# One buffer or two, by parity of the chunk, for the input of a depthwise convolution

## The reference, cut to what matters

```
zxbcdt = u @ in_w.T                       # 512 -> 1024 (z) + 1152 (xBC) + 16 (dt)
z, xBC, dt = split(zxbcdt)
xBC = conv1d(xBC, conv_w, depthwise, 4 taps, causal) + conv_b
xBC = silu(xBC)
xh, B, C = split(xBC)                     # 1024, 64, 64
state = dA * state + (dt * x) B^T;  y = C state      # per token, 16 heads of 64
y = (y + D * xh) * silu(z);  y = y * rsqrt(mean(y*y) + EPS) * rms_w
h = h + y @ out_w.T
```

## Time and profile before

| | us | share |
|---|---|---|
| median of three runs | 4825.02 | |
| profiled execution | 4828.47 | |
| its span | 4826.7 | |
| TensorE matmuls busy | 4096.1 | 85% |
| TensorE weight loads busy | 3622.3 | 75% |
| VectorE busy | 3357.0 | 70% |
| ScalarE busy | 2922.8 | 61% |
| GpSimd busy | 2002.1 | 41% |

### The profile page before, as it was taken

One profiled execution on the slowest core, in us unless ns is written; L12 is line 12 of the kernel. 1 busy time (PEld: TensorE's weight loads), 2 busy tenths in 40 slices (PEclk: granted clock), 3 DMA queues, 4 the chain that ended last, 5 costly groups with the idle time before them and its releaser, 6 DMA issues. The chain is left out here.

```text
span 4826.7 us, 100096 instructions
## 1 busy us (share of the span) xinstructions
PE 4096.1 (85%) x38872; PEld 3622.3 (75%) x38872; DVE 3357.0 (70%) x5217; ACT 2922.8 (61%) x4904; POOL 2002.1 (41%) x1572
## 2 busy tenths in 40 slices
PE   4399888888889899956989898989898998499999
PEld 1388888888878788846878888888888888377777
DVE  7377777777777777745777777777777777466664
ACT  4466666666666666635666666666666666466664
POOL 7134333333333334421333343434343444466664
PEclk6699999999999999978999999999999999699999
DMA  8300000000000000020000000000000000322220
GB/s 310 105 27 28 28 28 28 28 28 28 28 28 28 28 28 28 23 73 26 28 28 27 28 27 28 27 28 27 28 27 28 27 29 28 110 83 88 83 87 36
DMA packets 108673, 220.99 MB, mean 46 GB/s; under 512 B 10760, under 2 KB 11272, under 8 KB 107272
## 3 DMA queue, kind: packets, MB, share of 16 engines
q1 hardware_dynamic: 108176, 214.25, 12.6%
HBM read 146.97 MB, written 67.24 MB: 44 GB/s over the span
## 5 line engine op out<-in xcount | busy, mean ns | idle before, releaser
L501 PE MATMUL l_ring<-l_u_hi,l_wi_lo 128*128 128x256 f32 x4608 | 1312.9, 285 | 81.0 <-ACT l_raw L742 72.4
L501 PE MATMUL l_ring<-l_u_lo,l_wi_hi 128*128 128x256 f32 x4608 | 1298.1, 282 | 0.0
L501 PE MATMUL l_ring<-l_u_hi,l_wi_hi 128*128 128x256 f32 x4608 | 1296.9, 281 | 0.0
L974 DVE SCALAR_TENSOR_TENSOR l_xc<-l_raw,l_prm,l_xc 128x256 f32<-128x256 f32 x1536 | 852.3, 596 | 232.6 <-ACT l_xc L751 214.4
L501 PEld LDWEIGHTS l_ring<-l_u_hi,l_wi_lo 128*128 128x128 f32 x4608 | 876.4, 190 | 105.7 <-ACT l_raw L742 85.9
L501 PEld LDWEIGHTS l_ring<-l_u_lo,l_wi_hi 128*128 128x128 f32 x4608 | 876.1, 190 | 8.9
L501 PEld LDWEIGHTS l_ring<-l_u_hi,l_wi_hi 128*128 128x128 f32 x4608 | 874.6, 190 | 0.0
L1149 POOL TENSOR_TENSOR l_g<-l_g 128x512 f32<-128x512 f32 (+2 forms) x384 | 347.0, 904 | 926.8 <-ACT l_g L812 906.7
L1120 POOL TENSOR_TENSOR l_rhs<-l_cum,l_small 32x1024 fp32r<-32x1024 f32 x256 | 496.3, 1939 | 514.8 <-PE l_wide L563 474.1
L1006 DVE TENSOR_TENSOR l_e<-l_e,l_ps_m 128x1024 f32<-128x1024 f32 x256 | 312.8, 1222 | 414.2 <-ACT l_e L800 410.2
L501 PE MATMUL l_ring<-l_wo_hi,l_g_lo 128*128 128x512 f32 x1024 | 411.9, 402 | 82.9 <-DVE l_g_lo L1026 82.9
(11 more groups left out here) (162 smaller groups left out, 8335.2 us busy)
## 6 DMA issues: line engine op xcount, KB each, us to landing
l_hn<-h_scratch SPq DMA_DIRECT2D x64, 512.0 KB, 4.0
l_res<-h_scratch SPq DMA_DIRECT2D x128, 256.0 KB, 3.8
h_scratch<-l_res SPq DMA_DIRECT2D x128, 256.0 KB, 2.1
m_rows<-in_x SPq DMA_DIRECT2D x16, 1024.0 KB, 9.5
h_scratch<-m_rows SPq DMA_DIRECT2D x16, 1024.0 KB, 7.7
f_x<-in_x SPq DMA_DIRECT2D x16, 1024.0 KB, 6.1
f_h<-h_scratch SPq DMA_DIRECT2D x16, 1024.0 KB, 8.2
out<-f_x SPq DMA_DIRECT2D x64, 256.0 KB, 2.0
```

Source lines behind the costliest of these rows:

```text
L501: last = nc.tensor.matmul(out, a, c, start=(k == 0), stop=(k == n - 1))
L974: ins = nc.vector.scalar_tensor_tensor(out=acc, in0=raw[:, k, tap:tap + TB], scalar=prm_sb[:, w:w + 1], in1=acc, op0=ALU.mult, op1=ALU.add)
```

## The change

`raw` gets a dimension of two ahead of the others: [128, 2, 2, 259]. A chunk uses the half `(s + c) % 2`. As a step has five chunks and a sequence four steps, this is the parity of m, so neighbouring chunks have different halves. `conv_in` waits for `s_acc >= m - 1`, the taps of the chunk before the last, in place of `s_acc >= m`. Nothing else is changed: the order on each engine and all other waits stay.

```diff
-        raw = sb("raw", [P, 2, TB + TAPS - 1])
+        raw = sb("raw", [P, 2, 2, TB + TAPS - 1])
...
-                act.wait_ge(s_acc, m)
+                act.wait_ge(s_acc, at_least_0(m - 1))
                 if s == 0:
-                    nc.scalar.mul(raw[:, 0:nt, 0:TAPS - 1], small[:, 0:nt * 3].rearrange("p (k t) -> p k t", k=nt),
+                    nc.scalar.mul(raw[:, (s + c) % 2, 0:nt, 0:TAPS - 1], small[:, 0:nt * 3].rearrange("p (k t) -> p k t", k=nt),
                                   0.0).then_inc(s_halo, 1)
                 else:
                     act.wait_ge(s_halo2, m - (NX + 1) + 1)
-                    nc.scalar.copy(raw[:, 0:nt, 0:TAPS - 1], halo[:, t0:t0 + nt, :]).then_inc(s_halo, 1)
+                    nc.scalar.copy(raw[:, (s + c) % 2, 0:nt, 0:TAPS - 1], halo[:, t0:t0 + nt, :]).then_inc(s_halo, 1)
...
-                nc.scalar.copy(raw[:, 0:nt, TAPS - 1:], src_ps).then_inc(s_inev, 1)
+                nc.scalar.copy(raw[:, (s + c) % 2, 0:nt, TAPS - 1:], src_ps).then_inc(s_inev, 1)
...
-                    ins = nc.scalar.activation(acc_bc if c == 0 else xc[:, t0 - 1 + k, :], raw[:, k, 0:TB],
+                    ins = nc.scalar.activation(acc_bc if c == 0 else xc[:, t0 - 1 + k, :], raw[:, (s + c) % 2, k, 0:TB],
...
-                            out=acc, in0=raw[:, k, tap:tap + TB], scalar=prm_sb[:, w:w + 1], in1=acc,
+                            out=acc, in0=raw[:, (s + c) % 2, k, tap:tap + TB], scalar=prm_sb[:, w:w + 1], in1=acc,
```

## The result

Four runs of the changed kernel took 4616.07 to 4621.96 us, median 4619.05; four of the kernel before in the same comparison had 4825.90. The ratio is 0.957 (0.9555 to 0.9588): 207 us less. The prediction was 4633, the range 4612 to 4712. The profiled execution has a span of 4614.2 us, 212.5 less. The forecast's own narrower range, 4620 to 4652, misses the result by 1 us; what holds is the wider margin down to 4612.

The account below looks back on a forecast made before the run. No engine is full; raw's single buffer ties ScalarE and VectorE into a zigzag, with TensorE in the chain. Terms gave 2.85 to 3.2 us per step, taken as 3.1; 62 x 3.1 = 192 off 4825.0 gives 4633, range 4612 to 4712.

Parts of the forecast that it names:

- The wait attributed: ScalarE, chunks 3 and 4: conv_in waits for VectorE's taps (s_acc), though the view names TensorE; no size of its own.
- Chunk 2, 0.94 per step: conv_in starts 3.28 us earlier, so TensorE's wait before the states product goes: 0.94 us per step.
- Chunk 3, 1.10 per step: conv_in's copy comes earlier, so TensorE's wait before projection group 8 goes: 1.10 us per step.
- Chunk 4, 0.81: conv_in waits for group 8's end instead of taps 3: 1360.83 - 1360.02, within a start 3.0 us earlier.
- Sum: Whole kernel: 62 steps x 3.1 us = 192 us saved, from 4825.0 to 4633.
- upper bound of 3.2 per step: Highest gain per step: 3.0 by the transposes' start, plus about 0.1 for each of two TensorE restarts.
- Where it does not act: First step's chunks before each layer's loop (silu_x waits for the same taps) and each layer's last step: no gain.
- The lock: GpSimd and two-SBUF-input VectorE instructions share a port pair exclusively; the later blocks: 1.5 us for a caught tap.
- the addresses: Second buffer and tensors behind raw, moved 2072 bytes: cost taken as 0; slower reads feared, 5% chance, up to 4907.
- the register form of the wait: One more subtraction in the loop for conv_in's wait: at most some 0.1 us in chunk 2, taken as 0.
- Rival 2: Taps 4: one more tap waits for a GpSimd addition, 1.5 us more; step wins 1.6, 99 us, 4726; 7%.

Follow-up runs that it names:

- first experiment: Changed kernel with both halves of raw kept, but conv_in waiting again for the taps of the chunk before (s_acc >= m): 4829.2 us, ratio 1.0004.
- last experiment: Changed kernel with silu_x 4 and the exponential moved earlier on ScalarE, plus silu_x c behind conv_in c + 1 before each layer's loop: 4501.2 us, ratio 0.933.

## Why the prediction was right, and what it had too small

The forecast's mechanism is the one that ran, and the median lies 14 us below it. Its steps:

- *The wait attributed.* ScalarE's L739 was said to wait for taps where the view named TensorE. The first experiment leaves all but the wait as in the changed kernel and gives the old time, and chunk 3 alone gives 136 us: that is shown.
- *Chunk 2, 0.94 per step.* Measured 1.19: the square sum before stood at 1349.65, now at 1286.70 + 61.76 = 1348.46. The term missed a second, small wait: before, the outputs product stood 1.25 behind the states product (1347.32 in the earlier trace rows),

```profile
1348.57 1.15 PE L589 MATMUL l_ps_y<-l_e,l_xs 128*64 128x64 f32 x32
```

  after only 0.98, because VectorE's second product L1009 was late as well. The list of waits from 1000 to 2000 us had it under weight loads alone, before:

```profile
PEld l_ps_y L589 <- DVE l_e L1009: 7.9, 33, 0.2
```

  Chunk 2 by itself gave 78 us, where 0.94 gives 58 and 1.19 gives 74.
- *Chunk 3, 1.10 per step.* Measured 1.43: the transposes come 1359.86 - 1357.24 = 2.62 earlier, 1.19 of it from chunk 2. The row of a wait counts idle time from the modelled end of the last matmul, and these rows of before show what that leaves out:

```profile
1355.55 0.28 PE L501 MATMUL l_ring<-l_u_hi,l_wi_hi 128*128 128x256 f32 x1
1356.93 0.39 PE L501 MATMUL l_ring<-l_u_hi,l_wi_lo 128*128 128x256 f32 x1 [1.10 <-ACT l_raw L742]
1357.16 0.28 PE L501 MATMUL l_ring<-l_u_lo,l_wi_hi 128*128 128x256 f32 x1
```

  Inside a group the matmuls start 0.12 apart. Without the wait the group could have started at 1355.67, 0.16 before the modelled end, and its second matmul would stand 0.12 and not 0.23 behind the first: 1.10 + 0.16 + 0.11 = 1.37 of the 1.43. The prediction had allowed about 0.1 for this at each restart.
- *Chunk 4, 0.81.* Measured 3.39 - 2.62 = 0.77. The size was right, its cause was not: the prediction put it down to chunk 4's own looser wait. With chunks 2 and 3 alone loosened, `conv_in` 4 still waits for taps 3 and loses nothing, since these come earlier by chunk 3's change.
- *Sum.* 1.19 + 1.43 + 0.77 = 3.39 per step against 3.1 (the steady step is 3.40 shorter), and 62 x 3.39 = 210 against 192; the medians have 207, the profiled executions 212.5. The upper bound of 3.2 per step was too low by about the outputs' wait; the result is in the range because a margin was left down to 4612, 3.4 per step.
- *Where it does not act.* The start of a layer has the same gaps after as before. The reason given, `silu_x` in front, holds for a third of them; behind it stand the projection groups (last experiment). Of the two last steps without a convolution one kept its length (48.41, 48.30), the other lost 1.8 us (48.44, 46.63). In the trace with chunks 2 and 3 alone loosened they take 47.40 and 48.86, so they scatter by such amounts; the reason is open.
- *The lock, the addresses, the register form of the wait.* Taps 4 still take 2.71 in the changed kernel. Rival 2 priced a caught tap at 1.5 us of a step; where it happened the shift was 0.5 net, since `split_u` was then spared, and the clock came on top. And the first experiment's time leaves nothing for the addresses. It says nothing of the subtraction, which it does not have; in the changed kernel chunk 2's `conv_in` starts at 1276.77, when L812 (1275.81 + 1.06) is just over, so no cost shows there.

## What to carry to other kernels

What a single buffer between two engines costs cannot be read from its total of waits, but from what stands behind the waiting instruction: follow one step in order of time and ask at each removed wait what comes late next. Loosening one wait can make a second one worthless, so a list of gains taken one by one (263 us) is not their sum (207). Once a buffer is free, the same method on what is left of the in-order queues, an exponential put ahead of two copies, gave another 90 us without any more memory. Moving an instruction on a third engine can cost more than the sum of the shifts, here by the clock: read the granted clock step by step before putting a difference down to one cause.

## What had not been expected of the hardware

A removed wait of TensorE was worth 0.1 to 0.3 us more than its idle time in the profile in two places: 1.43 for 1.10 before group 8, and 1.57 for 1.32 before the states and 0.11 before the outputs. The order of two instructions on ScalarE decided which instructions of VectorE GpSimd's additions met: six taps of 2.71 us in all became 4.33, while `split_u` fell from 1.79 to 0.68. And a wait of 1.57 to 1.8 us in TensorE's queue, in place of two of 0.71 and 0.28, went with a fall of the granted clock to half in 28 steps of 47, at about 1.5 us each.
